# Attention kernel: unscaled probabilities, one of two query blocks turned by VectorE and moved through DRAM, inverse sums multiplied in after the value product

## The chip, the cores and the metric

The kernel runs on one core of a Trainium2 chip. The metric is the device time of that core in microseconds; it is the median of several executions. Beside it there is one profiled execution, from which every row below comes. "PE" is TensorE, "DVE" VectorE, "ACT" ScalarE, "POOL" GpSimd and "SP" SyncE, which only issues DMAs here.

## What is computed

The input is one sequence of 8192 tokens of width 512, all in 32-bit floats. It is layer-normalised, and the result goes through two branches that are added to the input:

```python
xn = layernorm(x)
x  = x + attention(xn) + feed_forward(xn)
# attention: 16 heads of 32 columns; a query block of 128 tokens sees the
# block before it, its own and the block after it (384 keys), banded
scores = einsum('bhnqd,bhnkd->bhnqk', qb, kwin) / sqrt(512)
scores = where(mask, scores, -1e30)
attn   = softmax(scores, axis=-1)
out    = einsum('bhnqk,bhnkd->bhnqd', attn, vwin) @ Wout + bout
```

The feed-forward branch (a ternary weight matrix up to 2048, a square of the positive part, and down again) is the first stage of the kernel. It writes its sum to a DRAM tensor `partial` and the transposed, normalised input to a DRAM tensor `xT`. The change does not touch it.

## The kernel before

The second stage, `attention_stage` (line 662), works on tiles of two query blocks, 32 tiles in all (`NT`). A tile is done in four steps (`c` = 0 to 3), each for four heads, which is one chunk of 128 of the 512 columns. There are 128 steps (`STEPS`), numbered `t`; `b` is the query block in the tile, `h` the head in the chunk, `u = 4b + h`. Each engine has its own program, a fixed list of instructions that loops over `t`; semaphores tie the programs together, and within an engine nothing overtakes. The order within a step is therefore written out by hand.

TensorE (lines 1252 to 1266) does in step `t`: `scores(t, 0)`; then four quarters, each `turn_probs(t-1, 1, part)` followed by a quarter of job A, the query and key projection for step `t+2` (24 matmuls of 256 columns, L1105); then `scores(t, 1)`; then `probs_times_values(t-1)` (L1217); then four quarters, each `turn_probs(t, 0, part)` followed by a quarter of job B, a projection of values (L1114) or the output product (L1123), 12 matmuls of 512 columns. `turn_probs` (L1193) is the transpose, on TensorE, of one head's 128 x 384 probabilities: three 128 x 128 transposes into one of two PSUM banks.

VectorE (lines 1069 to 1083) does `find_max` (L1006: masks a head's scores, scales them and finds the row maximum), `normalise` (L1017 reciprocal of the row sums of a pair of heads, L1021 multiplication of a head's probabilities by them, for three heads in four), `qk_low` (L1034, L1038), `oT_low` (L1027) and, in two steps of four, `add_out` (L1048). ScalarE (lines 977 to 994) does `exp` (L928, with the row sums as an accumulated output and a short instruction that reads them), `copy_pT` (L938: a head's turned probabilities from PSUM to SBUF, 384 columns), `qk_high` (L954, L957), `oT_high` (L946) and, in two steps of four, `take_v` (L921). GpSimd (lines 903 to 912) multiplies the fourth head's probabilities (L888), copies keys (L894, L895) and adds the output bias (L899). SyncE loads `xT` (L840), loads `partial` (L846) and stores the output (L850).

`job_ps` has two banks that jobs A, the value product and B take in turn. `wait_job_bank` makes each wait until the job two before it has been taken out: job B of a step waits for `qk_low` of the same step, job A of the next for the value product's `oT_low`.

Of the kernel before, what the change touches and what calls it, by code (L numbers as in the profile page):

```python
# [661 lines left out]
def attention_stage(nc, loaded, xT_dram, partial, out):  # L662
# [6 lines left out]
    VR = 6  # L669
    XR = 3  # L670

    ctx = ExitStack()
    with ctx:
# [27 lines left out]
        pT = wqkv_raw[:, 2:4, :].rearrange("p a (h w k) -> p (a h) w k", w=6, k=P)  # L701
        oT_hi = sb("oT_hi", [P, 2, DC, T], F32R)
        oT_lo = sb("oT_lo", [P, 2, DC, T], F32R)
# [21 lines left out]
        normalised, last_head_normalised = sem("normalised"), sem("last_head_normalised")  # L725
# [3 lines left out]
        oT_hi_done, oT_done = sem("oT_hi_done"), sem("oT_done")  # L729
# [40 lines left out]

        def job_a(t):
            return t + 2 if t + 2 < STEPS else None
# [19 lines left out]
        def job_release(n):  # L792

            t, k = divmod(n, 3)
            if k == 0:
                return (qk_done, job_a(t) + 1) if job_a(t) is not None else None
            if k == 1:
                return (oT_done, t) if 1 <= t <= STEPS else None
# [33 lines left out]
        def _(sp):  # L832
# [14 lines left out]

            def store_y(i, b):
# [8 lines left out]
            for i in range(NT + 1):  # L857
                if 1 <= i:
                    for b in range(2):
                        store_y(i - 1, b)  # L860
                        if i < NT:
                            load_part(i, b)
                if i + XR - 1 < NT:
                    load_x(i + XR - 1)
            for b in range(2):
                sp.wait_ge(y_stored[b], 16 * NT)

        @block.gpsimd
        def _(pool):
# [13 lines left out]
            def normalise_last_head(t, b):  # L883
                i, _ = where(t)
                cols = window(i, b)
                u = b * HC + HC - 1
                pool.wait_ge(rcp_done, 2 * (2 * t + b) + 2)
                nc.gpsimd.tensor_scalar(probs[:, u, cols], probs[:, u, cols], sum_rcp[:, u:u + 1], None, ALU.mult  # L888
                                        ).then_inc(last_head_normalised, 1)
# [13 lines left out]
            for t in range(STEPS + 3):  # L903
# [3 lines left out]
                if t < STEPS:  # L907
                    normalise_last_head(t, 0)
                if job_a(t) is not None and where(job_a(t))[0] % 2 == 0:
                    copy_keys(job_a(t))  # L910
                if t < STEPS:
                    normalise_last_head(t, 1)
# [3 lines left out]
        def _(act):  # L916
            def take_v(i, r, number, bank):
                act.wait_ge(job_filled, number)
                if i >= 2:
                    act.wait_ge(pv_done, 4 * i - 4)  # L920
# [10 lines left out]
            def copy_pT(t, b, h):  # L931
                i, _ = where(t)
                seen = blocks_seen(i, b)
                first = 3 * at(i, b)
                act.wait_ge(turned, 8 * t + b * HC + h + 1)
                if t >= 1:
                    act.wait_ge(pv_done, t)
                nc.scalar.copy(pT[:, h, first + seen.start:first + seen.stop, :].rearrange("p w t -> p (w t)"),  # L938
                               pT_ps[:, h % 2, seen.start * P:seen.stop * P]).then_inc(pT_done, 1)

            def oT_high(t):
                i, c = where(t)
                act.wait_ge(pv_done, t + 1)
                if i >= 2 and c == 0:
                    act.wait_ge(job_filled, B_NUMBER[4 * (i - 1) + 2])
                nc.scalar.copy(oT_hi[:, i % 2, c, :], job_ps[:, pv_bank(t), 0:T]).then_inc(oT_hi_done, 1)  # L946
# [30 lines left out]
            for t in range(STEPS + 3):  # L977
# [3 lines left out]
                for h in range(HC):  # L981
                    if 1 <= t <= STEPS:
                        copy_pT(t - 1, 1, h)
# [4 lines left out]
                for h in range(HC):  # L988
                    if t < STEPS:
                        exp(t, 1, h)  # L990
                    if h == 0 and 1 <= t <= STEPS:
                        oT_high(t - 1)
                    if t < STEPS:
                        copy_pT(t, 0, h)

        @block.vector
        def _(dve):
            def find_max(t, b):
# [3 lines left out]
                if t >= 1:  # L1002
                    dve.wait_ge(turned, 8 * (t - 1) + HC * (b + 1))
# [6 lines left out]
            def normalise(t, b):  # L1010
                i, _ = where(t)
                cols = window(i, b)
                for pair in range(2):
                    first = b * HC + 2 * pair
                    heads = slice(first, first + 2)
                    dve.wait_ge(exped, 8 * t + first + 2)
                    nc.vector.reciprocal(sum_rcp[:, heads], prob_sum[:, heads]).then_inc(rcp_done, 1)  # L1017
                    dve.wait_ge(rcp_done, 2 * (2 * t + b) + pair + 1)
                    for u in range(first, first + 2):
                        if u % HC < HC - 1:  # L1020
                            nc.vector.tensor_scalar(probs[:, u, cols], probs[:, u, cols], sum_rcp[:, u:u + 1], None,  # L1021
                                                    ALU.mult).then_inc(normalised, 1)

            def oT_low(t):
                i, c = where(t)
                dve.wait_ge(oT_hi_done, t + 1)
                nc.vector.tensor_tensor(oT_lo[:, i % 2, c, :], job_ps[:, pv_bank(t), 0:T],  # L1027
                                        oT_hi[:, i % 2, c, :].bitcast(F32), ALU.subtract).then_inc(oT_done, 1)
# [40 lines left out]
            for t in range(STEPS + 3):  # L1069
# [3 lines left out]
                if t < STEPS:  # L1073
                    find_max(t, 0)
                    normalise(t, 0)
# [11 lines left out]
        def _(pe):  # L1087
# [30 lines left out]
            def project_out(i, b, bank, first, last_):  # L1118
                for n in range(first, last_):
# [3 lines left out]
                    last = nc.tensor.matmul(job_ps[:, bank, :], a[:, i % 2, k, at(i, b) * P:(at(i, b) + 1) * P],  # L1123
# [58 lines left out]
            def turn_probs(t, b, h):  # L1182
                i, _ = where(t)
                u = b * HC + h
                n = 8 * t + u
                if n >= 2:
                    pe.wait_ge(pT_done, n - 1)
                if h == HC - 1:
                    pe.wait_ge(last_head_normalised, 2 * t + b + 1)
                else:  # L1190
                    pe.wait_ge(normalised, (HC - 1) * (2 * t + b) + h + 1)
                for w in blocks_seen(i, b):
                    last = nc.tensor.transpose(pT_ps[:, h % 2, w * P:(w + 1) * P], probs[:, u, w * P:(w + 1) * P],  # L1193
                                               ident[:, :])
                last.then_inc(turned, 1)

            def probs_times_values(t):
# [5 lines left out]
                pe.wait_ge(pT_done, 8 * t + 2 * HC)  # L1203
                parts = []
                for blk in (2 * i, 2 * i + 1):
                    first, second = (3 * place + blk - (2 * i - 1 + at(i, place)) for place in range(2))
                    parts.append((blk, slice(0, 2), slice(first, second + 1, second - first)))
                for b, blk in enumerate((2 * i - 1, 2 * i + 2)):
                    if 0 <= blk < NBLK:
                        place = at(i, b)  # L1210
                        seen = 3 * place + 2 * b
                        parts.append((blk, slice(place, place + 1), slice(seen, seen + 1)))
                for n, (blk, places, seen) in enumerate(parts):
                    for h in range(HC):
                        head = c * HC + h
                        strip = slice(h * DH, (h + 1) * DH)
# [136 lines left out]
```

## Time and profile before

| | us |
|---|---|
| median of three runs (2626.28 to 2631.04) | 2630.59 |
| the profiled execution, its own time | 2629.41 |
| span of its profile, first to last instruction | 2627.6 |
| around the span | 1.8 |

The page of the profile has the busy time of each engine, then the span in 40 equal slices with the busy share of each in tenths, the granted TensorE clock and the DMA traffic; then the chain of work that ended last; then groups of instructions. The feed-forward stage takes about the first 17 slices, the attention stage the rest. The same trace also answers for a single stretch of time: which engine was busy for how long in it, who waited for whom, and the instructions in order of time.

### The profile page before, as it was taken

To read this page: it belongs to the slowest core of one execution; us is meant where nothing else is said; L and a number is where in the kernel's file an instruction comes from. 1 tells how busy PE (TensorE), PEld (TensorE's weight loads), DVE (VectorE), ACT (ScalarE), POOL (GpSimd) and SP (SyncE) were. 2 spreads that over 40 slices of the span, in tenths; PEclk is the share of its full clock that TensorE was granted. 3 is DMA by queue.
4 is the path that set the end of the run, shared out by engine and by line. 5 is a ranking of instruction groups with operands and counts; after the bars stand their busy time and mean duration, and the time that the engine had idled before them with its cause. 6 is when DMAs were issued, how large, how long until landed. Compare 5 with 4: busy or idle time off the path is not lost.

```text
span 2627.6 us, 55989 instructions
## 1 busy us (share of the span) xinstructions
PE 2576.2 (98%) x19728; PEld 2090.2 (80%) x19728; DVE 1592.0 (61%) x4779; ACT 1638.1 (62%) x4260; POOL 631.8 (24%) x595
## 2 busy tenths in 40 slices
PE   6999999999999999989999999999999999999998
PEld 4888888888888888868888888888888888888885
DVE  5444444444444444357777777777777777777775
ACT  6333333333333333358888888888888888888886
POOL 0011111111111111033333333333333333333332
PEclk7999999999999999999999999999999999999999
DMA  5422222222222222021121111112111111112110
GB/s 181 146 80 81 80 80 80 80 80 80 80 80 80 80 80 64 33 81 34 34 65 34 53 46 42 58 41 58 34 61 39 42 58 42 58 34 65 34 46 29
DMA packets 188361, 167.43 MB, mean 64 GB/s; under 512 B 11328, under 2 KB 143424, under 8 KB 187632
## 3 DMA queue, kind: packets, MB, share of 16 engines
q1 hardware_dynamic: 188000, 164.41, 20.2%
q8 instruction: 132, 2.16, 0.4%
q14 instruction: 85, 0.70, 0.1%
q0 software_dynamic: 144, 0.17, 0.0%
HBM read 97.43 MB, written 67.11 MB: 63 GB/s over the span
## 4 chain that ended last, share of the span: by engine, by line
PE 55%; ACT 1%; issue 0%; DVE 0%; POOL 0%; POOLq 0%; ACTq 0%
PE pT_ps L1193 14%; PE job_ps L1105 14%; PE score_ps L1176 7%; PE job_ps L1123 7%; PE job_ps L1217 7%; PE job_ps L1114 7%; ACT wqkv_raw L928 1%; ACT wqkv_raw L938 0%; PE job_ps L1237 0%; PE score_ps L1227 0%; DVE wqkv_raw L1006 0%; DVE k_lo L1038 0%; ACT q_hi L954 0%; ACT k_hi L957 0%; POOL wout_raw L899 0%
## 5 line engine op out<-in xcount | busy, mean ns | idle before, releaser
L928 ACT ACTIVATE wqkv_raw<-wqkv_raw,neg_max 128x384 f32<-128x384 f32 (+1 forms) x1024 | 633.3, 619 | 186.3 <-DVE neg_max L1006 181.5
L888 POOL TENSOR_SCALAR wqkv_raw<-wqkv_raw,sum_rcp 128x384 f32<-128x384 f32 (+1 forms) x256 | 372.9, 1457 | 960.1 <-DVE sum_rcp L1017 960.1
L494 ACT ACTIVATE relu<-up_ps,fc_scale 128x512 f32<-128x512 f32 x256 | 176.2, 688 | 656.2 <-PE up_ps L625 656.2
L938 ACT COPY wqkv_raw<-pT_ps 128x384 f32<-128x384 f32 (+1 forms) x1024 | 484.7, 474 | 74.4 <-PE pT_ps L1193 74.1
L1193 PE MATMUL pT_ps<-ident,wqkv_raw 128*128 128x128 f32 x3040 | 513.4, 277 | 8.1 <-ACT wqkv_raw L938 7.7
L1006 DVE CUSTOM_DVE_ANT_0 wqkv_raw<-score_ps,mask 128x384 f32<-128x384 f32 (+1 forms) x1024 | 503.5, 548 | 5.7 <-PE score_ps L1176 1.6
L568 DVE SCALAR_TENSOR_TENSOR sq<-up_ps,relu 128x512 f32<-128x512 f32 x256 | 177.0, 692 | 531.8 <-ACT relu L494 530.4
L1193 PEld LDWEIGHTS pT_ps<-ident,wqkv_raw 128*128 128x128 f32 x3040 | 360.0, 140 | 119.1 <-ACT wqkv_raw L938 42.6
L635 PE MATMUL down_ps<-proj_T,sq_hi 128*128 128x512 f32 x1024 | 408.9, 399 | 0.9 <-DVE sq_lo L551 0.9
L637 PE MATMUL down_ps<-proj_T,sq_lo 128*128 128x512 f32 x1024 | 404.3, 395 | 0.0
L621 PE MATMUL up_ps<-f_xT_hi,fc_T 128*128 128x512 f32 x1024 | 399.2, 390 | 1.4 <-DVE low L539 1.4
L623 PE MATMUL up_ps<-f_xT_lo,fc_T 128*128 128x512 f32 x1024 | 399.2, 390 | 0.0
L1105 PE MATMUL job_ps<-xT_hi,wqkv_hi 128*128 128x256 f32 x1024 | 329.0, 321 | 0.1
L1021 DVE TENSOR_SCALAR wqkv_raw<-wqkv_raw,sum_rcp 128x384 f32<-128x384 f32 (+1 forms) x768 | 298.2, 416 | 17.9
L1017 DVE RECIPROCAL sum_rcp<-prob_sum 128x2 f32<-128x2 f32 x512 | 85.0, 166 | 354.5 <-ACT wqkv_raw L928 354.0
L1105 PE MATMUL job_ps<-xT_hi,wqkv_lo 128*128 128x256 f32 x1024 | 287.9, 281 | 0.0
L1105 PE MATMUL job_ps<-xT_lo,wqkv_hi 128*128 128x256 f32 x1024 | 287.8, 281 | 0.0
L454 POOL TENSOR_TENSOR f_y<-f_y,part_in 128x512 f32<-128x512 f32 x64 | 86.9, 1389 | 665.1 <-DVE f_y L559 665.1
L635 PEld LDWEIGHTS down_ps<-proj_T,sq_hi 128*128 128x128 f32 x1024 | 193.4, 189 | 43.9 <-DVE sq_lo L551 2.2
L621 PEld LDWEIGHTS up_ps<-f_xT_hi,fc_T 128*128 128x128 f32 x1024 | 192.3, 188 | 44.0 <-DVE low L539 2.2
L637 PEld LDWEIGHTS down_ps<-proj_T,sq_lo 128*128 128x128 f32 x1024 | 193.0, 188 | 43.0
L623 PEld LDWEIGHTS up_ps<-f_xT_lo,fc_T 128*128 128x128 f32 x1024 | 192.3, 188 | 42.5
(126 smaller groups left out, 4228.2 us busy)
## 6 DMA issues: line engine op xcount, KB each, us to landing
xT_hi<-xT SPq DMA_DIRECT2D x65, 256.0 KB, 3.8
xT_lo<-xT SPq DMA_DIRECT2D x65, 256.0 KB, 4.5
f_x_in<-in_L_attn_x SPq DMA_DIRECT2D x64, 256.0 KB, 3.2
xT<-f_xT_hi SPq DMA_DIRECT2D x64, 256.0 KB, 2.6
xT<-f_xT_lo SPq DMA_DIRECT2D x64, 256.0 KB, 2.8
part_in<-in_L_attn_x SPq DMA_DIRECT2D x64, 256.0 KB, 3.4
partial<-f_y SPq DMA_DIRECT2D x64, 256.0 KB, 2.0
wout_raw<-partial SPq DMA_DIRECT2D x64, 256.0 KB, 2.8
```

Source lines behind the costliest of these rows:

```text
L621: nc.tensor.matmul(up_ps[:, s % 2, :], fc_T[:, k, cols], xT_hi[:, par, k, :], start=(k == 0), stop=False)
L623: nc.tensor.matmul(up_ps[:, s % 2, :], fc_T[:, k, cols], xT_lo[:, par, k, :], start=False, stop=False)
L635: nc.tensor.matmul(down_ps[:, b, :], sq_hi[:, s % 2, t], proj_T[:, s, :], start=(s == 0), stop=False)
L637: last = nc.tensor.matmul(down_ps[:, b, :], sq_lo[:, s % 2, t], proj_T[:, s, :], start=False, stop=(s == FB - 1))
L888: nc.gpsimd.tensor_scalar(probs[:, u, cols], probs[:, u, cols], sum_rcp[:, u:u + 1], None, ALU.mult).then_inc(last_head_normalised, 1)
L928: nc.scalar.activation(probs[:, u, cols], probs[:, u, cols], ACT.Exp, bias=neg_max[:, u:u + 1], scale=-1.0, accum_out=prob_sum[:, u:u + 1] ...
L938: nc.scalar.copy(pT[:, h, first + seen.start:first + seen.stop, :].rearrange("p w t -> p (w t)"), pT_ps[:, h % 2, seen.start * P:seen.stop ...
L1006: nc.vector.tensor_tensor_reduce(out=probs[:, u, cols], in0=score_ps[:, h, cols], in1=mask[:, cols], scale=-SCORE_SCALE, scalar=3e38, op0= ...
L1021: nc.vector.tensor_scalar(probs[:, u, cols], probs[:, u, cols], sum_rcp[:, u:u + 1], None, ALU.mult).then_inc(normalised, 1)
L1105: last = nc.tensor.matmul(job_ps[:, bank, is_k * T:(is_k + 1) * T], w[:, k, col:col + P], tokens, start=(m == 0), stop=(m == PASSES * DC - 1))
L1114: last = nc.tensor.matmul(job_ps[:, bank, :], a[:, k, x_slot(i) + r, :], w[:, k, 2 * D:3 * D], start=(n == 0), stop=(n == PASSES * DC - 1))
L1193: last = nc.tensor.transpose(pT_ps[:, h % 2, w * P:(w + 1) * P], probs[:, u, w * P:(w + 1) * P], ident[:, :])
```

## The change

Probabilities are no longer multiplied by the inverse row sums. Instead the transposed output `oT`, [columns of the chunk x tokens], is multiplied by a transposed, widened table of them:

- `normalise` (DVE) and `normalise_last_head` (POOL) are gone. `inverse_sums` takes one reciprocal of four heads for each block, two in a step. `widen_inverse_sums` (POOL) copies each to a 128 x 128 table, in which each head's column stands 32 times.
- Block `b = 1` is turned on TensorE as before (`turn_probs(t, h)`, in job A's quarters of the next step). Heads 2 and 3 get a fourth transpose each, of the two widened tables; `copy_pT` then copies 512 columns in place of 384.
- Block `b = 0` is not turned on TensorE. `turn_blocks` (DVE) transposes the 32 x 32 blocks of each head's 128 x 384 probabilities into `blocks`. SyncE writes `blocks` to DRAM in one DMA (`move_blocks_out`), waits until it has landed, and reads it back in four DMAs of 32 partitions each (`move_blocks_in`) into `pT_moved`, which completes the transposition. Both directions go in contiguous pieces of 512 bytes, 12 for each of 128 partitions. `blocks`, `pT_moved` and `pT` exist once each; `turned_dram` twice.
- The value product has six parts of 128 columns for each head (three key blocks for each query block) in place of two of 256 and two of 128. Block 0's parts read `pT_moved` in runs of 32 elements that lie 128 elements apart.
- New on DVE: `scale_oT`, the product's 128 x 256 times the turned table, PSUM and SBUF to SBUF; `oT_high` and `oT_low` read its result. On ACT `oT_high` comes after all exponentials. `values` has 5 blocks in place of 6, `oT_hi` and `oT_lo` 6 places of one chunk in place of two tiles.
- The output stores and the loads on SyncE now stand behind a step's moves.

```diff
@@ SyncE @@
+            def move_blocks_out(t):
+                ...
+                sp.wait_ge(blocks_turned, HC * (t + 1))
+                if first == 0:
+                    sp.dma_start(moved.rearrange("a w p x -> p (a w) x"),
+                                 blocks.rearrange("p a w h t -> p (a w) (h t)")).then_inc(blocks_out, 16)
+                ...
+            def move_blocks_in(t):
+                ...
+                sp.wait_ge(blocks_out, 16 * transfers_out(t + 1))
+                if t >= 1:
+                    sp.wait_ge(pv_done, t)
+                for a in range(STRIPS):
+                    moved = turned_dram[t % 2 * STRIPS + a, first:3, :, :].rearrange("w (q j) x -> j (w q) x", j=DH)
+                    sp.dma_start(pT_moved[a * DH:(a + 1) * DH, first:3, :, :, :].rearrange("j w q h t -> j (w q) (h t)"),
+                                 moved).then_inc(blocks_moved, 16)
...
+            for t in range(STEPS + DC):
+                i, c = where(t)
+                if t < STEPS:
+                    move_blocks_out(t)
+                    move_blocks_in(t)
+                if c == 1 and i + XR - 1 < NT:
                     load_x(i + XR - 1)
+                if c >= 2 and i >= 1:
+                    store_y(i - 1, c - 2)
+                    if i < NT:
+                        load_part(i, c - 2)
@@ GpSimd @@
-            def normalise_last_head(t, b):
+            def widen_inverse_sums(t, b):
+                pool.wait_ge(rcp_done, 2 * t + b + 1)
+                if t >= 1:
+                    pool.wait_ge(turned, HC * t)
+                heads = slice(b * HC, (b + 1) * HC)
+                nc.gpsimd.tensor_copy(rcp_wide[:, b, :, :], sum_rcp[:, heads].unsqueeze(2).to_broadcast([P, HC, DH])
+                                      ).then_inc(rcp_widened, 1)
@@ ScalarE @@
                 for h in range(HC):
                     if t < STEPS:
                         exp(t, 1, h)
-                    if h == 0 and 1 <= t <= STEPS:
-                        oT_high(t - 1)
-                    if t < STEPS:
-                        copy_pT(t, 0, h)
+                if 1 <= t <= STEPS:
+                    oT_high(t - 1)
@@ VectorE @@
                 if t < STEPS:
                     find_max(t, 0)
-                    normalise(t, 0)
+                    for u in range(HC):
+                        turn_blocks(t, u)
+                    inverse_sums(t, 0)
                 if job_a(t) is not None:
                     qk_low(job_a(t), a_bank(t))
                 if t < STEPS:
                     find_max(t, 1)
                 if 1 <= t <= STEPS:
+                    scale_oT(t - 1)
+                if t < STEPS:
+                    inverse_sums(t, 1)
+                if 1 <= t <= STEPS:
                     oT_low(t - 1)
-                if t < STEPS:
-                    normalise(t, 1)
@@ TensorE @@
                 for w in blocks_seen(i, 1):
                     last = nc.tensor.transpose(pT_ps[:, h % 2, w * P:(w + 1) * P], probs[:, u, w * P:(w + 1) * P],
                                                ident[:, :])
+                if h >= HC - 2:
+                    place = h - (HC - 2)
+                    pe.wait_ge(rcp_widened, 2 * t + 2)
+                    last = nc.tensor.transpose(pT_ps[:, h % 2, 3 * P:4 * P],
+                                               rcp_wide[:, at(i, place), :, :].rearrange("p h t -> p (h t)"), ident[:, :])
...
+                pe.wait_ge(blocks_moved, 16 * STRIPS * (t + 1))
+                pe.wait_ge(pT_done, HC * (t + 1))
...
                 for part in range(QUARTERS):
-                    if t < STEPS:
-                        turn_probs(t, 0, part)
                     run_b(t, part)
```

## Rows read from the trace of the kernel before

**Rows 1.** The page: busy time, then PE's slices and its granted clock.

```profile
PE 2576.2 (98%) x19728; PEld 2090.2 (80%) x19728; DVE 1592.0 (61%) x4779; ACT 1638.1 (62%) x4260; POOL 631.8 (24%) x595
...
PE   6999999999999999989999999999999999999998
...
PEclk7999999999999999999999999999999999999999
```

**Rows 2.** Busy time by stretch: stretch, length, busy (instructions) by engine, clock, DMA share, GB/s.

```profile
1150.00:2620.00 1470.00, 1457.93 (x14692) 1183.92 (x14691) 1064.48 (x3773) 1196.91 (x3517) 496.05 (x446) 1.00 0.15 45
```

**Rows 3.** Who waited for whom, 1150 to 2620 us: us in total, times, longest.

```profile
ACT wqkv_raw L928 <- DVE neg_max L1006: 181.5, 131, 1.4
...
PEld pT_ps L1193 <- ACT wqkv_raw L938: 42.6, 140, 1.5
```

**Rows 4.** PE of one step in order of time: start, us, work.

```profile
1801.77 0.45 PE L1176 MATMUL score_ps<-k_hi,q_hi 32*128 32x384 f32 x4
...
1802.50 0.55 PE L1193 MATMUL pT_ps<-ident,wqkv_raw 128*128 128x128 f32 x3
...
1803.47 0.28 PE L1105 MATMUL job_ps<-xT_hi,wqkv_lo 128*128 128x256 f32 x1
1803.60 0.49 PE L1193 MATMUL pT_ps<-ident,wqkv_raw 128*128 128x128 f32 x3
1803.84 0.36 PE L1105 MATMUL job_ps<-xT_hi,wqkv_hi 128*128 128x256 f32 x1
1804.04 0.28 PE L1105 MATMUL job_ps<-xT_lo,wqkv_hi 128*128 128x256 f32 x1
1804.16 0.28 PE L1105 MATMUL job_ps<-xT_hi,wqkv_lo 128*128 128x256 f32 x1
...
1807.53 1.51 PE L1217 MATMUL job_ps<-wqkv_raw,values 128*32 128x256 f32 x32
1808.96 0.55 PE L1193 MATMUL pT_ps<-ident,wqkv_raw 128*128 128x128 f32 x3
...
1813.21 0.45 PE L1176 MATMUL score_ps<-k_hi,q_hi 32*128 32x384 f32 x4
```

**Rows 5.** PE in order of time, inside one value product.

```profile
1807.53 1.07 PE L1217 MATMUL job_ps<-wqkv_raw,values 128*32 128x256 f32 x16
...
1808.43 0.60 PE L1217 MATMUL job_ps<-wqkv_raw,values 128*32 128x128 f32 x14
```

**Rows 6.** ACT of the same step in order of time.

```profile
1806.20 0.48 ACT L938 COPY wqkv_raw<-pT_ps 128x384 f32<-128x384 f32 x1
1806.58 0.62 ACT L928 ACTIVATE wqkv_raw<-wqkv_raw,neg_max 128x384 f32<-128x384 f32 x1
1807.10 0.19 ACT L928 ACTIVATION_READ_ACCUMULATOR wqkv_raw<-wqkv_raw,neg_max 128x1 f32 x1
...
1807.54 0.47 ACT L957 ACTIVATE k_hi<-job_ps,qk_bias 128x256 fp32r<-128x256 f32 x1
```

**Rows 7.** DVE of the same step in order of time.

```profile
1805.44 0.75 DVE L1021 TENSOR_SCALAR wqkv_raw<-wqkv_raw,sum_rcp 128x384 f32<-128x384 f32 x2
...
1808.45 0.48 DVE L1038 SCALAR_TENSOR_TENSOR k_lo<-job_ps,qk_bias,k_hi 128x256 fp32r<-128x256 f32 x1
1808.84 0.55 DVE L1006 CUSTOM_DVE_ANT_0 wqkv_raw<-score_ps,mask 128x384 f32<-128x384 f32 x1
...
1809.32 0.55 DVE L1006 CUSTOM_DVE_ANT_0 wqkv_raw<-score_ps,mask 128x384 f32<-128x384 f32 x1
...
1810.75 0.42 DVE L1027 TENSOR_TENSOR oT_lo<-job_ps,oT_hi 128x256 fp32r<-128x256 f32 x1
```

**Rows 8.** Groups of POOL, 1150 to 2620 us: busy, mean ns, idle before.

```profile
L894 POOL CAST k_hi<-k_hi 128x256 fp32r<-128x256 f32 x64 | 25.1, 392 | 9.2 <-DVE k_lo L1038 9.2
```

**Rows 9.** Line 411, 600 to 1000 us: stores of 512 pieces of 512 bytes.

```profile
DMA to landing us min/median/max: 2.6/2.7/3.1
```

**Rows 10.** Line 840: loads of 512 pieces of 512 bytes, issued four together.

```profile
L840 SPq DMA_DIRECT2D xT_lo<-xT x65: 617/631/830, 1132.3 to 2517.3; - x65
...
DMA to landing us min/median/max: 3.2/4.2/6.4
```

**Rows 11.** Busy time by stretch, while line 411's stores run back to back.

```profile
60.00:62.00 2.00, 2.00 (x6) 1.25 (x6) 0.00 (x0) 0.00 (x0) 0.00 (x0) 0.50 1.04 286
```

More of the change, by code:

```diff
@@ L929, in exp, with copy_pT @@
                                      accum_out=prob_sum[:, u:u + 1]).then_inc(exped, 1)
[L931 removed]
+            def copy_pT(t, h):
                 i, _ = where(t)
[L933 to L935 removed]
+                seen = blocks_seen(i, 1)
+                last = 4 if h >= HC - 2 else seen.stop
+                act.wait_ge(turned, 4 * t + h + 1)
                 if t >= 1:
[L937 to L939 removed]
+                    act.wait_ge(oT_scaled, t)
+                nc.scalar.copy(pT[:, h, seen.start:last, :].rearrange("p w t -> p (w t)"),
+                               pT_ps[:, h % 2, seen.start * P:last * P]).then_inc(pT_done, 1)
             def oT_high(t):
                 i, c = where(t)
[L943 to L946, printed above, removed]
+                act.wait_ge(oT_scaled, t + 1)
+                if i >= 1 and c == OR - DC:
+                    act.wait_ge(job_filled, B_NUMBER[4 * i + 2])
+                nc.scalar.copy(oT_hi[:, t % OR, :], oT[:, :]).then_inc(oT_hi_done, 1)
             def qk_high(u, number, bank):
@@ L1008, in find_max, with inverse_sums @@
                                                    accum_out=neg_max[:, u:u + 1]).then_inc(maxed, 1)
-            def normalise(t, b):
-                i, _ = where(t)
[L1012 to L1022, printed above, removed]
+            def inverse_sums(t, b):
+                heads = slice(b * HC, (b + 1) * HC)
+                dve.wait_ge(exped, 8 * t + (b + 1) * HC)
+                if t >= 1:
+                    dve.wait_ge(rcp_widened, 2 * (t - 1) + b + 1)
+                nc.vector.reciprocal(sum_rcp[:, heads], prob_sum[:, heads]).then_inc(rcp_done, 1)
@@ new lines, in turn_blocks @@
+            def turn_blocks(t, u):
+                i, _ = where(t)
+                seen = blocks_seen(i, 0)
+                dve.wait_ge(exped, 8 * t + u + 1)
+                if u == 0 and t >= 1:
+                    dve.wait_ge(blocks_out, 16 * transfers_out(t))
+                nc.vector.transpose(blocks[:, :, seen.start:seen.stop, u, :].rearrange("p a w t -> p w a t"),
+                                    probs[:, u, seen.start * P:seen.stop * P].rearrange("p (w a t) -> p w a t", a=STRIPS, t=DH)
+                                    ).then_inc(blocks_turned, 1)
@@ L1202, in probs_times_values @@
                     pe.wait_ge(v_done, min(2 * i + 3, NBLK))
[L1203 to L1216, printed above, removed]
-                        last = nc.tensor.matmul(job_ps[strip, bank, places.start * P:places.stop * P],
-                                                values[:, blk % VR, head * DH:(head + 1) * DH], pT[:, h, seen, :],
-                                                start=(n == 0), stop=(n == len(parts) - 1), tile_position=(0, h * DH))
+                pe.wait_ge(blocks_moved, 16 * STRIPS * (t + 1))
+                pe.wait_ge(pT_done, HC * (t + 1))
+                for b in range(2):
+                    seen = blocks_seen(i, b)
+                    for w in seen:
+                        blk = 2 * i - 1 + b + w
+                        for h in range(HC):
+                            head = c * HC + h
+                            strip = slice(h * DH, (h + 1) * DH)
+                            cols = slice(at(i, b) * P, (at(i, b) + 1) * P)
+                            out_ = job_ps[strip, bank, cols].rearrange("p (q t) -> p q t", t=DH)
+                            p = pT[:, h, w, :].rearrange("p (q t) -> p q t", t=DH) if b else pT_moved[:, w, :, h, :]
+                            last = nc.tensor.matmul(out_, values[:, blk % VR, head * DH:(head + 1) * DH], p,
+                                                    start=(w == seen.start), stop=(w == seen.stop - 1),
+                                                    tile_position=(0, h * DH))
                 last.then_inc(pv_done, 1)
```

96 lines of the change are left out of this document (54 added, 42 removed).

## The prediction

> **What bounds the kernel now.** I read the page first: PE is busy for 98% of the span, in every slice after the first, at the full granted clock [rows 1]. The change touches the attention stage alone. There PE is busy for 1457.93 of 1470 us, ACT for 1196.91 (81%), DVE for 1064.48 (72%), and the DMA engines for a share of 0.15 at 45 GB/s [rows 2]. Then the waits: the largest on PE is its weight loads' wait for `copy_pT`, 42.6 us in all; ACT waits 181.5 us for maxima, which costs nothing as long as PE does not wait [rows 3]. So the stage lasts as long as PE's instructions. A step goes from score to score, 1813.21 - 1801.77 = 11.44 us [rows 4], and 128 of them are 1464 us. What the change is worth is read from one step: what PE loses, and whether what it then waits for comes in time. I count from the start of `scores(t, 0)` as 0.
>
> **PE's own work.** Eight turns go out of a step's list, four stay. Between two matmuls of job A the pace is 1804.16 - 1804.04 = 0.12 us; across a turn and the slower first matmul behind it (0.20 in place of 0.12) it is 1803.47 to 1804.04 for two matmuls, 0.57 us [rows 4]. A turn so costs 0.57 - 2 x 0.12 = 0.33 us, and each of its three transposes 0.11. Four turns less is -1.31 us. The two transposes of the widened tables add 2 x 0.11 = 0.22 us.
>
> The value product keeps its 768 columns for each head but in six parts of 128. A round of four heads takes (1.07 - 0.38) / 3 = 0.23 us where it has 256 columns and (0.60 - 0.27) / 3 = 0.11 where it has 128 (the first and last start in a row of the trace, less the length of one matmul, over three rounds) [rows 5]. Two times six rounds at 0.11 are 1.31 us against 1.43 for the whole product before (1808.96 - 1807.53) [rows 4]. I take 0. The strided reads of `pT_moved` have no row: the nearest is the two-block read of the 256-column parts, with no visible cost; at worst, if they ran at half pace, half of the product would cost 0.65 us more. That end is in the range only.
>
> PE's work is then 11.44 - 1.31 + 0.22 = 10.35 us. If nothing else bound, 128 x 1.09 = 139.5 us would go: 2491.
>
> **What PE then waits for: job B's bank.** Job B used to have a turn ahead of it; now it follows the product directly. In the old step the product starts at 5.76; two added transposes put it at 5.98 and B at 7.41. B needs `qk_low` to have emptied job A's bank, at 1808.45 + 0.48 = 7.16 before [rows 7]. That moves too. The last `copy_pT` begins 0.22 later (4.65 in place of 4.43) and, with 512 columns, holds ACT for 0.38 + 0.12 = 0.50 in place of 0.38 (starts of copy and exponential) [rows 6], so the last exponential starts at 5.15 in place of 4.81, its sum is out at 5.86, and `k_hi` ends at 6.58. On DVE the last `turn_blocks` waits for that sum: 5.9 to 6.35; the reciprocal follows, 6.5, and `qk_low` takes 6.62 to 7.5. PE waits 0.1 to 0.15 us for it. In the two steps of four that have `add_out` DVE starts the maxima about 0.6 late; about 0.15 of that reaches the last exponential. I take 0.2 on the mean.
>
> The DVE transpose has no row in the old trace. Below it lies the multiplication it replaces, 0.375 us a head (0.75 for two); above it, far off, an elementwise instruction of more columns, 128 x 512 for 0.68 (`add_out`'s size, an estimate from the 0.48 us maxima pace of 384 columns scaled to 512 is 0.64) [rows 7]. I take 0.45, near the row of equal size. Only the last of four lies on the path, since the others fit between exponentials a microsecond apart: the ends are worth -0.08 and +0.23 us a step, -10 and +29 us in all. Here a page speaks against the change. The Trainium skill (VectorE: DVE Perf Modes, The three transpose paths) gives 311 ns for a 128 x 128 bf16 transpose on VectorE; three such are 0.93 us a head. No row shows one; it is priced as a rival below, by rows.
>
> **DVE and ACT as a loop.** `find_max(t, 1)` runs from 7.5 to 9.5 (pace 1809.32 - 1808.84 = 0.48) [rows 7]; the four exponentials start at 8.1 and, 0.61 apart, end at 10.7; `scale_oT` (0.42, the length of `oT_low`) fits in between; then the reciprocal of block 1 makes DVE wait until 10.9. Queued behind it are `oT_low` (until 11.3), `add_out` and the next `find_max`, which PE's scores would allow at 10.35 + 0.85 = 11.2. The loop is as long as PE's step to about 0.1 us: counted above. DVE's work falls (six multiplications at 0.375, four transposes and one scaling in their place) and so does ACT's (four copies at 0.38 less). POOL loses two multiplications and gets two copies; the widening of 128 columns is bounded above by the 0.39 us of a 256-column copy [rows 8], and it is wanted for the third turn, some 1.9 us after the reciprocal. Nothing.
>
> **The way through DRAM.** Block 0 of step t is turned at 6.4. Its product is due in the next step, at 5.98 + 10.55 = 16.5. In those 10.1 us it must be written and read. A store of 512 pieces of 512 bytes lands after 2.7 us [rows 9]. While such stores ran back to back, the 16 engines moved 286 GB/s at a share of 1.04 [rows 11]: 512 pieces are 0.92 us, 1536 (786,432 bytes) 2.75. So out is 2.7 - 0.92 + 2.75 = 4.5 us. In is four issues, 0.63 us each on SP [rows 10], the last at 1.9; the row for four such loads together says 3.2 to 6.4 to landing, with 2048 pieces where these have 1536. I take 4.9. The data is there at 6.4 + 9.4 = 15.8, 0.7 us early. `move_blocks_in` also waits for the product before, over at 7.4, long before the store lands. Existing DMAs now queue behind these on SP: the output's stores and `load_x`, 2048 pieces or 3.7 us of the engines in one step of four. These delay the next step's store by about 1 us, and so the product by 0.3 once in four: 0.1 a step. SP itself is held for about 4.5 + 4 x 0.63 + 2.5 = 9.5 of 10.5 us in that step; what it delays then is the next store, within the same 1 us. Load of the DMA engines: 2 x 2.75 + 0.15 x 11.44 = 7.2 us of 10.6, 68%.
>
> Here too a page speaks against it. The Trainium skill (SBUF — State Buffer, Door 1: The DMA port swizzle) says that a transfer of 32 partitions reaches 8 of 16 ports, about 218 GB/s; then the reads would take 3.6 us in place of 2.75. No run here shows such a transfer. By it the data would be 0.2 us late, not 0.7 early: some 10 to 20 us more.
>
> **The sum.** 10.35 + 0.2 + 0.05 = 10.6 us a step, 0.84 less than 11.44; 128 x 0.84 = 107 us. From the profiled execution's own 2629.4 (span 2627.6 and 1.8 around it, 1.2 below the median of the runs) that is 2522, from the median 2523. I give 2525.
>
> **The rivals.**
> 1. Slow transfers (slower than before). What decides is the time L from `scores(t, 0)` to the data's landing. If the product waits s in every step, the next scores move by s as well, and both products in between wait: L = 5.98 + 10.35 + 2s. So s = (L - 16.33) / 2. A step is as long as before at s = 1.09, L = 18.5: out and in together take 12.1 us in place of 9.4. For it: short pieces scattered over DRAM in steps of 64 KB where the rows show pieces that lie together, four reads that wait for a fresh write, and loads that took up to 6.4 us [rows 10]. Against it: the engines are free two thirds of the time now. Price, if a piece took 1.75 times as long: 13.6 us, L = 20, s = 1.85, a step of 12.2: 2630 + 128 x 0.76 = 2727.
> 2. A long transpose on DVE. At twice the pace of the maxima, 0.95 us: the last one ends at 6.85, `qk_low` at 7.9, PE waits 0.5 us; the maxima of block 1 and all behind them move by the same, and the loop of the part before comes out at 10.85 to 11.05. Then 2560 to 2580; I take 2575. That is what the page of the Trainium skill cited for the transpose would make of it.
> 3. The transfers are just late, L near 18: 2600 to 2635, gain eaten up.
> 4. PE alone binds, nothing of the above is seen: 2491 to 2500.
>
> **How the numbers follow.** Forecast (2505 to 2555) 0.43; DVE loop 0.18; slow transfers 0.23; just late 0.09, of which about half lies within 0.2% of before or close to it; PE alone 0.07. 0.2% (5 us) is about what a measurement of this kernel can tell from no change. Faster by more: 0.43 + 0.18 + 0.07 + 0.05 = 0.73; within: 0.04; slower: 0.23. The range goes from 2495, which leaves half of the last case out, to 2680, which takes in the slow case up to s = 1.5: about 0.15 is left out. The forecast's own range is 2505 to 2555.
>
> **What would show it.** In the new trace: steps of 10.6 us; turns on PE half as many, with the value product still about 1.4 us; the product's wait for a DMA near zero, and near 1 to 2 us in each of 128 steps if rival 1 holds; job B's first matmul waiting 0.1 to 0.3 us for `k_lo`, 0.5 or more under rival 2; `turn_blocks` at about 0.45 us; the store's landing at 4.5 us and the last read's at 3; the DMA share near 0.68. Wrong would be the sum if PE waits somewhere that I did not name, above all if scores wait for maxima (the DVE loop), or if one of the moved pieces costs much more than the 29 ns on an engine that 286 GB/s over 16 engines make of 512 bytes.

## The result, and the profile after

The changed kernel takes 2592.88 us (median of four runs, 2584.47 to 2599.21), the one before 2630.47: a ratio of 0.9858, 95% interval 0.9826 to 0.9891. It is faster by 38 us where 105 were forecast. The profiled execution is the slowest of the four, 2599.21 us: what is read from its trace is up to 6.3 us, or 0.05 us a step, above the median.

The page, as in [rows 1], first: PE's busy share has fallen from 98 to 95%, the DMA engines, at 1 or 2 tenths in the attention stage before, are now at 7 in most slices.

```profile
PE 2464.5 (95%) x20512; PEld 2034.7 (78%) x20512; DVE 1589.0 (61%) x4395; ACT 1493.8 (58%) x3748; POOL 339.0 (13%) x595
...
DMA  4422222222222222125777776777777777777765
```

Then busy time in a stretch of the attention stage, with the columns of [rows 2]. In 1200 us PE is idle for 68.7.

```profile
1250.00:2450.00 1200.00, 1131.26 (x13092) 948.80 (x13092) 898.86 (x2852) 888.31 (x2528) 172.84 (x376) 1.00 0.73 190
```

The store of the turned blocks (L865) stands once in each step: instructions with the least, median and greatest duration in ns, the first and the last start, and the times from issue to landing.

```profile
L865 SPq DMA_DIRECT2D turned_blocks<-wqkv_raw x124: 370/376/1157, 1203.9 to 2571.6; - x124
...
DMA to landing us min/median/max: 4.1/4.7/7.3
```

The mean step is so (2571.6 - 1203.9) / 123 = 11.12 us, where [rows 4] had 11.44, and PE is idle for 68.7 / (1200 / 11.12) = 0.64 us of it. 11.12 - 0.64 is 10.48. The gain on PE's list is there, as forecast: 11.44 - 10.48 = 0.96 us a step. Two thirds of it, 0.64, are waited away again. Who waits for whom, as in [rows 3], says where:

```profile
PEld job_ps L1270 <- issue: 112.4, 126, 3.6
...
PE job_ps L1270 <- issue: 59.3, 54, 2.3
...
DVE wqkv_raw L1045 <- PE score_ps L1229: 44.6, 34, 3.7
...
PE job_ps L1270 <- DMA wqkv_raw<-turned_blocks: 18.3, 21, 3.4
PEld job_ps L1167 <- DVE k_lo L1087: 10.7, 31, 1.4
```

The value product (L1270) is what waits: its weights' loads 112.4 us and its matmuls 59.3 + 18.3. Most is put down to "issue", which names nothing; only 18.3 us name the reads from DRAM. The experiments show that it is those. Job B's wait for `k_lo` is small (10.7), and scores wait hardly ever.

One step in which the product does not wait, PE in order of time, to hold against [rows 4]:

```profile
1825.83 0.45 PE L1229 MATMUL score_ps<-k_hi,q_hi 32*128 32x384 f32 x4
...
1831.87 0.86 PE L1270 MATMUL job_ps<-wqkv_raw,values 128*32 128x128 f32 x24
1832.52 0.87 PE L1270 MATMUL job_ps<-pT,values 128*32 128x128 f32 x24
1833.37 0.50 PE L1167 MATMUL job_ps<-wqkv_hi,xT_hi 128*128 128x512 f32 x1
...
1836.36 0.45 PE L1229 MATMUL score_ps<-k_hi,q_hi 32*128 32x384 f32 x4
```

It is 10.53 us long, from scores to scores. The product begins at 6.04 (forecast 5.98), job B at 7.54 (7.5). DVE of the same step:

```profile
1831.71 0.58 DVE L1062 STREAM_TRANSPOSE wqkv_raw<-wqkv_raw 128x384 f32<-128x384 f32 x1 [0.58 <-ACT wqkv_raw L967]
1832.21 0.14 DVE L1054 RECIPROCAL sum_rcp<-prob_sum 128x4 f32<-128x4 f32 x1
...
1832.84 0.47 DVE L1087 SCALAR_TENSOR_TENSOR k_lo<-job_ps,qk_bias,k_hi 128x256 fp32r<-128x256 f32 x1
```

And SyncE's DMA issues from the step before on; each step has one store and four reads:

```profile
1820.40 0.37 SPq L865 DMA_DIRECT2D turned_blocks<-wqkv_raw  x1
1826.49 1.86 SPq L880 DMA_DIRECT2D wqkv_raw<-turned_blocks  x4
...
1832.31 0.37 SPq L865 DMA_DIRECT2D turned_blocks<-wqkv_raw  x1
1837.42 1.86 SPq L880 DMA_DIRECT2D wqkv_raw<-turned_blocks  x4
```

The store leaves at 1832.31 - 1825.83 = 6.48 (forecast 6.4). The reads follow 5.1 us later, 6.1 in the step before. A step that does wait, SyncE first:

```profile
1760.12 1.31 SPq L851 DMA_DIRECT2D xT_lo<-xT  x2
1762.13 0.39 SPq L865 DMA_DIRECT2D turned_blocks<-wqkv_raw  x1
1769.20 1.86 SPq L880 DMA_DIRECT2D wqkv_raw<-turned_blocks  x4
```

PE of the same step:

```profile
1775.17 0.86 PE L1270 MATMUL job_ps<-wqkv_raw,values 128*32 128x128 f32 x24 [2.29 <-issue]
```

Here the store went out 0.7 us after the last loads of `xT` and took 7.1 us; the reads took 6.0 until the product, which had waited 2.3 us.

Over the middle 108 steps of the trace, from a store's issue to the first read's is 4.97 us on the mean (4.6 in three steps of four, 6.05 in the one behind the loads of `xT`), and from the first read's issue to the product 6.2 us in the steps that wait; over all 108 the last read has landed 5.89 us after the first one's issue. The forecast had 4.5 and 4.9. The four reads are issued within 1.50 us, and the later one is issued, the longer it takes: 2.83, 3.40, 3.87 and 4.38 us on the mean.

### The profile page after: what moved, and what is told of

Its sections match the earlier page's. It is cut to its first block, busy times and chain, and to the rows that moved or that the text cites. A ratio compares the mean times of both kernels' runs of the same rounds, so it can differ in the third digit from the quotient of the medians.

```text
span 2597.4 us, 57215 instructions
## 1 busy us (share of the span) xinstructions
PE 2464.5 (95%) x20512; PEld 2034.7 (78%) x20512; DVE 1589.0 (61%) x4395; ACT 1493.8 (58%) x3748; POOL 339.0 (13%) x595
## 4 chain that ended last, share of the span: by engine, by line
PE 43%; DMA 6%; issue 4%; ACT 2%; SPq 1%; DVE 1%; POOLq 0%; POOL 0%
PE job_ps L1158 11%; PE job_ps L1176 7%; PE job_ps L1270 6%; PE pT_ps L1243 6%; PE job_ps L1167 6%; PE score_ps L1229 5%; DMA turned_blocks<-wqkv_raw 3%; DMA wqkv_raw<-turned_blocks 3%; ACT wqkv_raw L967 1%; SPq L880 1%; PE pT_ps L1248 1%; DVE wqkv_raw L1062 0%; PE job_ps L1290 0%; PE score_ps L1280 0%; DVE k_lo L1087 0%
## 5 line engine op out<-in xcount | busy, mean ns | idle before, releaser
L967 ACT ACTIVATE wqkv_raw<-wqkv_raw,neg_max 128x384 f32<-128x384 f32 (+1 forms) x1024 | 622.4, 609 | 183.9 <-DVE neg_max L1045 181.8
L1062 DVE STREAM_TRANSPOSE wqkv_raw<-wqkv_raw 128x384 f32<-128x384 f32 (+1 forms) x512 | 289.4, 570 | 170.4 <-ACT wqkv_raw L967 158.1
L977 ACT COPY pT<-pT_ps 128x384 f32<-128x384 f32 (+2 forms) x512 | 271.5, 530 | 146.9 <-PE pT_ps L1243 137.3
L1243 PE MATMUL pT_ps<-ident,wqkv_raw 128*128 128x128 f32 x1520 | 258.8, 279 | 1.3 <-ACT pT L977 1.3
L926 POOL COPY rcp_wide<-sum_rcp 128x128 f32<-128x128 f32 x256 | 74.9, 293 | 1101.5 <-DVE sum_rcp L1054 1101.5
L1243 PEld LDWEIGHTS pT_ps<-ident,wqkv_raw 128*128 128x128 f32 x1520 | 175.2, 141 | 34.6 <-issue 31.7
L1158 PEld LDWEIGHTS job_ps<-xT_lo,wqkv_hi 128*128 128x128 f32 x1024 | 196.4, 192 | 0.0
L1158 PEld LDWEIGHTS job_ps<-xT_hi,wqkv_hi 128*128 128x128 f32 x1024 | 196.0, 191 | 0.5 <-ACT values L960 0.3
```

The lines of the kernel that those rows point to most:

```text
L967: nc.scalar.activation(probs[:, u, cols], probs[:, u, cols], ACT.Exp, bias=neg_max[:, u:u + 1], scale=-1.0, accum_out=prob_sum[:, u:u + 1] ...
L977: nc.scalar.copy(pT[:, h, seen.start:last, :].rearrange("p w t -> p (w t)"), pT_ps[:, h % 2, seen.start * P:last * P]).then_inc(pT_done, 1)
L1062: nc.vector.transpose(blocks[:, :, seen.start:seen.stop, u, :].rearrange("p a w t -> p w a t"), probs[:, u, seen.start * P:seen.stop * P]. ...
L1158: last = nc.tensor.matmul(job_ps[:, bank, is_k * T:(is_k + 1) * T], w[:, k, col:col + P], tokens, start=(m == 0), stop=(m == PASSES * DC - 1))
```

## The experiments

Two theories stood after the result. A: the trip through DRAM is late, and each wait feeds back. L is the time from the start of a step's scores to the landing of its data, and "due" is when the product would start if PE never waited. A wait ahead of one product also delays the scores of the next step and with them its data, so s = (L - due) / 2, where s is the mean wait. B: another loop, of DVE and ACT or over job B's bank, is nearly as long, and the transfers hide it. In the table, all kernels are the changed one with one edit, `best` with three. Steps come from the first and last store's start, PE's idle time from 1250 to 2450 us, as above; both are of the profiled execution, so for differences between medians the first columns count.

| kernel | median us | ratio to before, 95% | step us | PE idle in it, us |
|---|---|---|---|---|
| changed | 2592.9 | 0.9858 (0.9826 to 0.9891) | 11.12 | 0.64 |
| no_wait | 2512.8 | 0.9563 (0.9543 to 0.9583) | 10.49 | 0.04 |
| b1_first | 2568.2 | 0.9771 (0.9755 to 0.9787) | 10.86 | 0.35 |
| exp_early | 2563.1 | 0.9739 (0.9718 to 0.9760) | 10.85 | 0.38 |
| x_spread | 2584.0 | 0.9834 (0.9815 to 0.9853) | 10.95 | 0.51 |
| light_x | 2566.4 | 0.9757 (0.9741 to 0.9773) | 10.86 | 0.38 |
| read_wide | 2578.9 | 0.9814 (0.9797 to 0.9832) | 10.96 | 0.46 |
| read_once | 2558.9 | 0.9733 (0.9712 to 0.9755) | 10.78 | 0.33 |
| write_twice | 2815.3 | 1.0705 (1.0671 to 1.0739) | 12.84 | 1.79 |
| best | 2520.9 | 0.9592 (0.9576 to 0.9608) | 10.50 | 0.06 |

**Is it the transfers?** `no_wait` keeps all of them and takes away what needs them.

```diff
-                pe.wait_ge(blocks_moved, 16 * STRIPS * (t + 1))
...
-  p = pT[:, h, w, :].rearrange(...) if b else pT_moved[:, w, :, h, :]
+  p = pT[:, h, w, :].rearrange(...) if b else pT[:, :, w, h * DH:(h + 1) * DH]
```

> The changed kernel, but block 0's part of the value product reads the table turned on TensorE (same shapes, runs of 32) and does not wait for the transfers, which all still run. It leaves out the use of block 0's own probabilities. Theory A (the product's wait for the transfers, 0.67 us in the mean step of 11.15, is what the forecast missed, and behind it the step is TensorE's 10.4 to 10.5): 0.67 x 128 = 85 us less than the changed kernel, some 8 us more from the clock drops that follow long waits: 2500. Theory B (the loop of VectorE and ScalarE or the wait for job B's bank lies close behind): the step falls only to 10.8 or so, 2545.

Measured: 2512.8, where the forecast's sum, with 0.05 us a step for the transfers, came to 2522. The same stretch:

```profile
1250.00:2450.00 1200.00, 1195.67 (x13924) 1001.38 (x13920) 945.29 (x3024) 936.74 (x2680) 183.74 (x400) 1.00 0.77 200
```

PE is idle for 4.3 of 1200 us, with the DMA engines as busy as ever (0.77). The wait for the transfers cost 80 us. Of the 85 us between the two profiled executions, 0.60 x 128 = 77 are PE's idle time. Theory B falls: nothing else binds above 10.49 us.

**Does a wait feed back?** The trace of the changed kernel shows how. A step's store leaves 6.48 to 6.49 us after its scores in all of the middle 108 steps, whether PE has waited or not: what delays the scores delays the data. From the scores to the step's own product PE's list takes 16.33 us by the forecast, and two waits lie in between, the one before that product and the one before the product ahead of it. Where the data is late these two together make L - 16.33. In the 58 steps where the product waits for over 0.3 us their sum is less than that by 0.11 us on the mean, with a standard deviation of 0.07. The two need not be equal: where one product has waited long, the next waits little.

Two kernels give the trip more room from its two ends. `b1_first` needs the data 0.65 us later:

```diff
-                pe.wait_ge(blocks_moved, 16 * STRIPS * (t + 1))
                 pe.wait_ge(pT_done, HC * (t + 1))
-                for b in range(2):
+                for b in (1, 0):
+                    if b == 0:
+                        pe.wait_ge(blocks_moved, 16 * STRIPS * (t + 1))
```

> The changed kernel with the value product's two halves in the other order: block 1, whose table comes from TensorE, first, and the wait for the transfers only ahead of block 0. That gives each transfer 0.65 us more. Theory A (the wait feeds back: every wait also delays the next scores, so s = (L - due) / 2): steps that wait gain 0.33 us, the mean step 0.25 to 0.3: 32 to 38 us, 2555 to 2560. Rival (no feedback, a plain offset): 0.5 to 0.65 us in each waiting step, 60 us or more: 2530.

Measured: 2568.2, 25 us less, which is 0.19 us a step by the medians and 0.26 by the traces, for 0.65 us of room. By itself this separates the two only weakly: barely more than half of the steps wait, so a plain offset would have given 0.35 us on the mean and not the 0.5 or more that was expected of it. `exp_early` sends the data off earlier; this is the order of ScalarE's calls in the first half of a step, written short:

```diff
-  copy(0) exp(0) copy(1) exp(1) copy(2) exp(2) copy(3) exp(3)
+  copy(0) exp(0) copy(1) exp(1) exp(2) copy(2) exp(3) copy(3)
```

> The changed kernel, with ScalarE's list in the first half of a step reordered: exponentials 2 and 3 of block 0 go ahead of copies 2 and 3 of block 1's turned probabilities, which wait for TensorE's turns. The last exponential then starts some 0.6 to 0.7 us earlier, and so do the store of block 0 and the query and key evictions behind it. Theory A (L counts from the scores through the last exponential, the store and the reads; s = (L - due) / 2): each waiting step gains 0.3, the mean step 0.25: 30 us, 2563, as much as from the later block 0 in b1_first. Rival (the trip on the DMA engines alone sets the pace, since they are busy for 0.7): no change, 2585 to 2595.

Measured: 2563.1, the 2563 expected. ScalarE in order of time:

```profile
1828.89 0.48 ACT L977 COPY pT<-pT_ps 128x384 f32<-128x384 f32 x1 [1.90 <-PE pT_ps L1243]
...
1831.98 0.62 ACT L967 ACTIVATE wqkv_raw<-wqkv_raw,neg_max 128x384 f32<-128x384 f32 x1
1832.50 0.19 ACT L967 ACTIVATION_READ_ACCUMULATOR wqkv_raw<-wqkv_raw,neg_max 128x1 f32 x1
```

The last exponential of block 0 starts 3.09 us after the first copy; in the changed kernel it was 1830.97 - 1827.14 = 3.83. 0.74 us of room gave 0.23 us a step by the medians, 0.27 by the traces. The third test goes the other way and makes the trip longer: `write_twice` stores block 0 twice, and the reads wait for both.

```diff
-                moved = turned_dram[t % 2 * STRIPS:(t % 2 + 1) * STRIPS, :, :, :]
+                for n in range(2):
+                    write_blocks(first, turned_dram[(2 * n + t % 2) * STRIPS:(2 * n + t % 2 + 1) * STRIPS, :, :, :])
```

> The changed kernel, full computation, with the store of block 0 made a second time to another DRAM place, and the reads waiting for both: 1536 pieces more, by the rate of 286 GB/s 2.75 us longer on the way, and every step now waits. Theory A (feedback, s = (L - due) / 2): L grows from 17.5 to 20.2, the wait s from 0.67 to about 1.95, the mean step from 11.15 to 12.4: 160 us more, 2750. Rival (no feedback: the whole 2.75 is added to each step): 13.8 us a step, 2900 or more. Rival 2 (the DMA engines become the bound, 3 x 2.75 + 1.7 = 10 us of 12.4): anything over 2800 with a DMA share near 1.

Measured: 2815.3. That lies between A's 2750 and the 2900 without feedback, and so misses both numbers; it is over rival 2's 2800.

```profile
1250.00:2450.00 1200.00, 1032.99 (x11409) 865.67 (x11408) 782.32 (x2484) 780.50 (x2204) 148.90 (x325) 0.95 0.84 226
```

PE's idle time is 1.79 us a step where A said 1.95. The time from the store to the reads grew by 2.86 us, the idle time only by 1.15. The products of four steps in a row show the two waits sharing one trip:

```profile
1755.25 1.51 PE L1273 MATMUL job_ps<-wqkv_raw,values 128*32 128x128 f32 x24 [3.93 <-issue]
...
1768.00 0.86 PE L1273 MATMUL job_ps<-wqkv_raw,values 128*32 128x128 f32 x24
...
1782.07 1.51 PE L1273 MATMUL job_ps<-wqkv_raw,values 128*32 128x128 f32 x24 [3.51 <-DMA wqkv_raw<-turned_blocks]
...
1795.07 0.86 PE L1273 MATMUL job_ps<-wqkv_raw,values 128*32 128x128 f32 x24
```

One product waits for 3.5 to 3.9 us, the next one for nothing. What A had left out of the time is the granted clock: it is 0.95 on the mean, so 10% of the time at 1.2 GHz in place of 2.4. That is worth up to 5% of 12.84, 0.64 us a step; without it the step would be 12.2 or a little more, where A had 12.4. The DMA share is 0.84 and not near 1, which speaks against rival 2.

**What makes the trip long?** Four kernels each take something out of it. `x_spread` issues the four loads of `xT` behind four steps' moves, `light_x` moves a quarter of their bytes:

```diff
-                if c == 1 and i + XR - 1 < NT:
-                    load_x(i + XR - 1)
+                piece = (c - 1) % DC
+                j = (t - 1) // DC + XR - 1
+                if t >= 1 and j < NT:
+                    load_x_piece(j, piece)
@@ light_x, in load_x @@
+                        ks = slice(0, 1 if j >= XR else DC)
-  sp.dma_start(xT[:, :, x_slot(j) + r, :]..., xT_rows(xT_dram, blk, hl))
+  sp.dma_start(xT[:, ks, x_slot(j) + r, :]..., xT_rows(xT_dram, blk, hl)[:, ks, :])
```

> The changed kernel with the four loads of xT, which now go out together behind the moves of one step in four, issued one behind each step's moves. Theory A (the step behind the loads waits 1.36 us where the steps c = 0 and 1 wait 0.5 to 0.7, because its store queues behind 2048 pieces): that excess goes, 0.7 us once in four steps: 22 us, 2570, and the store's trip of 6.05 us in that step falls to about 4.8. Rival (the DMA engines' load counts, not its bunching): the same bytes, the excess spreads over the four steps: no change within 8 us.

> The changed kernel with a quarter of each load of xT left out of use after the first three tiles (only one chunk of four is loaded, so a quarter of those bytes moves and the projections read old tokens in the rest): 1536 fewer pieces of 512 bytes in one step of four. Theory A (the store queues behind those loads; in x_spread the same load then met each step's moves, which is why only 9 of 22 us came): the wait at c = 2 falls from 1.36 to about 0.6 and the rest stays: 2565 to 2570. Rival (bytes of others do not matter): 2590.

By the medians `x_spread` gave 9 us, neither the 22 nor clearly none; the changed kernel's runs spread over 15 us, and between the two profiled executions it is 20. How much it gives stays open. The stores no longer have a long one (landing, line of the store in `x_spread`, against 7.3 at most above):

```profile
DMA to landing us min/median/max: 4.1/4.6/5.8
```

but now every step has 512 pieces more around its moves, which may be why not all of the 22 came. `light_x` gave 26 us, as A said. By its trace PE's idle time ahead of the product of `c` = 2, the one whose store is behind the loads, falls from 1.32 to 0.35 us; for `c` = 3, 0 and 1 it goes from 0.13, 0.46 and 0.63 to 0.27, 0.45 and 0.44. So three quarters of the loads' bytes cost 26 us.

`read_wide` and `read_once` move the same pieces of 512 bytes into other places:

```diff
-  moved = turned_dram[... + a, first:3, :, :].rearrange("w (q j) x -> j (w q) x", j=DH)
-  sp.dma_start(pT_moved[a * DH:(a + 1) * DH, first:3, :, :, :].rearrange("j w q h t -> j (w q) (h t)"), moved)
+  moved = turned_dram[... + a, first:3, :, :].rearrange("w p x -> p w x")          # read_wide, four times
+  sp.dma_start(pT_moved[:, first:3, a, :, :].rearrange("p w h t -> p w (h t)"), moved)
+  sp.dma_start(pT_moved..."p (w q) (h t)", turned_dram..."a w p x -> p (a w) x")   # read_once
```

> The changed kernel with the four reads over 128 partitions and 3 pieces of 512 bytes each, in place of 32 partitions and 12 pieces: same bytes, pieces and count of DMAs, other places, so the value product gets block 0's probabilities unturned. Theory P (a transfer to 32 partitions runs at a lower rate): the time from the first read's issue to the product falls from 6.2 to about 5.3 us, half of it comes off each waiting step: 2545 to 2555. Rival Q (what makes reads slow is fixed latency and queueing, not the partitions): 6.2 us stays within 0.2, 2585 to 2595.

> The changed kernel with one read of 128 partitions and 12 pieces of 512 bytes each in place of four: same bytes and pieces in one DMA, other places, so the product gets block 0's probabilities unturned. Against read_wide (2579, 5.8 us from the first read's issue to the product in waiting steps) it takes away three issues, 1.5 us on SyncE. Theory I (the last read is late because it is issued 1.5 us after the first): 5.8 falls to 4.6 or so, the mean step by 0.35: 2535. Theory B (the engines' transfer of 1536 pieces is the length, and the issues overlap it): no more than 0.4 less, 2565 to 2575.

`read_wide`: the landing of a read, first in the changed kernel, then here:

```profile
DMA to landing us min/median/max: 2.3/3.5/6.6
```

```profile
DMA to landing us min/median/max: 2.1/3.0/5.9
```

0.5 us less at the median, 0.4 less to the product (5.8 in the steps that wait), 14 us of time. Both theories named there miss. The edit changes the partitions that a read writes and also the order in which it takes the pieces from DRAM; which of the two counts was not separated. Together they are worth 0.4 to 0.5 us, half of the 0.85 that the partitions' rate alone would make. `read_once` takes 20 us more away, 34 in all, nearer to its theory B: three issues less are worth 0.16 to 0.18 us a step and not 0.35. Taken one by one, bytes of the loads of `xT` (26), places of the reads (14) and issues (20) make 60 of the 80 us; that they add up was not tried.

**The version that results.** `best` has the whole computation and three of the edits: `b1_first`, `exp_early`, `x_spread`.

> The changed kernel with three edits together, full computation: block 1 first in the value product, the xT loads spread over four steps, and exponentials 2 and 3 ahead of copies 2 and 3. Theory A: 0.65 + 0.65 us more room and 0.1 to 0.2 from the loads; from L - due = 1.2 on the mean nothing is left to wait for in most steps: 10.5 to 10.6 us a step, 2515 to 2525. Rival (gains overlap or the trip grows with the load of the DMA engines): 2540 to 2550.

Measured: 2520.9, faster than before by 4.1% (ratio 0.9592) and than the changed kernel by 72 us.

```profile
1250.00:2450.00 1200.00, 1192.81 (x13917) 999.43 (x13915) 947.81 (x3024) 923.14 (x2681) 184.87 (x400) 1.00 0.79 201
```

PE's idle time is 7.2 of 1200 us, and the whole time is 8 us above `no_wait`'s. Alone the edits gave 25, 30 and 9.

## Why the prediction was wrong, point by point

- **PE's own work** (11.44 - 1.31 + 0.22 + 0 = 10.35): right to 0.1 us. Steps without a wait are 10.49 to 10.55, and `no_wait`'s mean is 10.49, the wait for job B's bank included. The value product in six parts starts job B 1.50 us later, against 1.43; its two halves take 0.65 and 0.85, the reads in runs of 32 no longer than the others.
- **Job B's bank** (0.2): right in kind, smaller. In `no_wait` job B's first matmul comes 1.56 us after the product's, 0.1 above the 1.45 of steps where nothing holds it.
- **The DVE transpose** (0.45): 0.58 us long, but the reciprocal starts 0.50 after it; `k_lo` starts at 7.01 and ends at 7.48 (7.5). Rival 2 did not come. The estimate of 0.93 us a head, three times the 311 ns that the Trainium skill (VectorE: DVE Perf Modes, The three transpose paths) gives for a 128 x 128 bf16 transpose, is too long for this shape.
- **DVE and ACT as a loop**: right, it does not bind above 10.49.
- **The way through DRAM**: this step failed. "The data is there at 15.8, 0.7 us early" has L = 6.4 + 4.5 + 4.9. On the mean of the middle 108 steps it was 6.48 + 4.97 + 5.89 = 17.3, and 18.4 in the step behind the loads of `xT`, where the product is due at 16.5. The store's term was taken from stores alone; behind the loads it was 1.5 us longer in one step of four, where the text had about 1 and a price of 0.1 us a step, and the sum only 0.05. The reads' term was the greater miss, 1.0 us: it was chosen from a row that spans 3.2 to 6.4 [rows 10], because fewer pieces move. It was made of 1.9 us until the last read's issue and 3 until that one's landing; measured are 1.50 and 4.38. So not the issues but the last read's landing was mis-sized: it was taken as if the reads ahead of it were out of its way, and the four land later one after another, 2.83 to 4.38 us after their issue. Of the 1.4 us, 0.4 to 0.5 go with the 32 partitions and the order in DRAM (`read_wide`), for which the prediction had a sentence with 0.85 but no place in the sum. There the Trainium skill (SBUF — State Buffer, Door 1: The DMA port swizzle) has transfers to 32 partitions at a lower rate; the direction agrees with `read_wide`, the size is half of what the rate would make.
- **The feedback formula** of rival 1 held for the mean, but the prediction's "s in every step" did not: the waits are uneven, and with data that is late it is the sum of two in a row that L fixes. From the mean L it gives (17.3 - 16.33) / 2 = 0.5 against 0.64 idle; it is short because a step whose data is early gives nothing back. With the second store L is 20.2, which gives 1.94 against 1.79. The case that came nearest is rival 3, "just late, L near 18", 2600 to 2635, which got 0.09; 2593 itself lies in none of the cases. The mistake behind that chance: with a margin of 0.7 us out of a trip of 9.4, known to 1 or 2 us, the margin had nearly the same chance of either sign, and the chances gave lateness of any kind 0.32.
- **The clock** stood in no sum. In the changed kernel's profiled execution it costs up to (36.0 - 11.0) / 2 = 12 us more than before; see below.

## What to carry to other kernels

Where a round trip is to fit into a gap of a pipeline, compare its spread, not its median, with the margin, and write down the room as a term of the sum: here a trip that was 0.9 us too long on the mean, and 2 us in one step of four, took 0.6 us from the mean step. Before rebuilding the transfer, look for room at its two ends: which operand of the consumer can be used first, and which producer stands behind a wait that is not its own; two reorderings of a few lines were worth 25 and 30 us, each alone. Bulk loads issued just ahead of a transfer become part of its latency: from the store to the reads it took 6.05 us behind the loads of `xT` and 4.6 elsewhere, and 4.6 in every step of `light_x`, which loads a quarter of those bytes.

## What the runs showed of the hardware

The granted clock fell after some long waits of PE, though PE is busy for 95% of the span. Around the step above, the product had waited 2.29 us; two stretches:

```profile
1773.00:1776.00 3.00, 0.83 (x32) 0.86 (x36) 2.91 (x11) 1.58 (x6) 1.03 (x3) 1.00 1.09 328
1776.40:1779.70 3.30, 3.30 (x19) 2.34 (x11) 1.03 (x3) 1.32 (x5) 0.29 (x1) 0.50 0.42 125
```

After 3 us with 0.83 busy, the clock is at 0.50, 1.2 GHz, for 3.4 us of full work. Between 1250 and 2450 us this happened three times, after waits of 1.85, 1.88 and 2.29 us; twelve other waits of 1.5 to 2.3 us had no such stretch behind them, so the wait's length alone does not decide it. From 1210 us on there are 36.0 us of such stretches in the trace of the changed kernel, 26 of them in its last 60 us, where PE is often idle anyway; 5.4 in that of `no_wait`, 11.0 in that of the kernel before, and 203 with the store made twice. Each microsecond in them costs up to half a one. So a wait of 2 us can cost more than 2 us, which was not expected of a kernel whose PE is 95% busy.

The second thing is that 512-byte pieces kept their price: 1536 of them to DRAM places 64 KB apart landed after 4.1 us at least and 4.7 at the median, against 4.5 estimated from stores of 512 pieces. And the DMA engines, busy for 0.77 in `no_wait`, did not slow the others: an exponential took 612 ns there on the mean against 622 before, a maximum 551 against 552 and the matmuls of job A, by kind, 282 to 323 against 281 to 321.
